# A second set of buffers for the second layer's regrouped queries, keys and values

## The chip, the cores and the metric

The kernel runs on one core of one Trainium2 chip. The metric is the device time of one execution in microseconds; the median of three runs before the change is 618.75 us (617.87 to 620.15). Changes within about half a per cent can't be told from none.

## The reference

Two transformer layers over 2,048 tokens (2 x 1024) of width 256. What matters here:

```python
# layer 0: causal attention, 32 heads of width 8, 8 key/value heads, T = 1024; then a gated FFN, fp8 inputs
q = (x @ Wq + bq).reshape(B, T, 32, 8).transpose(0, 2, 1, 3)
...
out = softmax(mask(q @ k.T / sqrt(8))) @ v @ Wo + bo
ffn = fp8dot(gelu(fp8dot(xn, w_gating[0])) * fp8dot(xn, w_gating[1]), w_linear)
x = x + out + ffn
# layer 1: attention *across the heads of a token*, 16 heads of width 16, no mask
scores = jnp.einsum('bshd,bstd->bsht', q, k) / jnp.sqrt(jnp.float32(HD))
weights = jax.nn.softmax(scores, axis=-1)
attn = jnp.einsum('bsht,bstd->bshd', weights, v)
# beside it a SiLU-gated FFN with RMS norm in the middle and ternary weights; x + both is the output
```

In the first layer the attention and the FFN both start from the same normed input. In the second layer the attention mixes only the 16 heads of one token, so every token is a small 16 x 16 attention of its own.

## The kernel before

The 2,048 tokens are 16 tiles of 128 (NT = 16). Every stage is a small function of a tile number, one set of functions per engine: `xnT.5` on TensorE turns tile 5's normed input, `qkv.5` projects it, and so on. The five lists in `ORDER` (lines 46 to 175) say in which order each engine issues these steps; each list is the program of its engine, so the engines run only in that order. Each step begins with its waits (`w.wait_ge`) on the semaphores that the other engines count up. The lists interleave the two layers and many tiles: while the first layer's attention of a late tile runs (`qk.Q`, `exp.Q`, `pv.Q`, 144 quads of score banks), the second layer of an earlier tile goes on beside it.

The second layer's attention of tile n goes through these steps, and these are what the change touches:

- TensorE `qkv1` (lines 737, 738) projects; ScalarE `qk1c` (L939), VectorE `ro1`, `ro2`, `v1c` (L1319 to L1328, L1306) and GpSimd `ro1p` (L1588, L1590) rotate and copy the result to `rqkv`, which has two copies.
- SyncE's queue: `vw` (L492) writes `rqkv` to a scratch tensor in HBM, and `vr` (L500, three DMAs) reads it back regrouped: each partition then holds one head of 8 tokens, 16 groups, in the buffer `G3` (queries, keys and values). There is one `G3`. So `vr(n)` waits for `PV1(n-1)`, the last reader of `G3`.
- TensorE `gT.2n` and `gT.2n+1` (L742) turn the queries and the keys of `G3`; VectorE `gTq` (L1335) and ScalarE `gTk` (L946) copy them to `qk1T`. There is one `qk1T`, so both wait for `S1(n-1)`.
- TensorE `S1` (L775) makes the scores of 8 tokens at a time. A pair of rows and columns in `G3` (written once by `cst`, L1026, from `ind1`) adds a large negative number where query and key are of different tokens. ScalarE `ex1` (L955) writes the exponentials to `stage`, of which there is one, and TensorE `PV1` (L786) multiplies them by the values.
- `o1r` (L1352), `o1T` (L795), `o1` (L1358, L1361) copy, turn and divide; SyncE's `ow` (L505) and `at1r` (L511) go through HBM again to bring the tokens back to partitions; `at1T` (L563, L564), `at1Tc` (L1403) and `wo1` (L807, L808) end it, and `yo` (L1409) adds the residual.

The second layer's FFN of the same tile is `gu` (L821, four parts), ScalarE `tg` (L964), VectorE `sg`, `hh` (L1368, L1377), then `ssq` (L970), `ssm` (L1383), `rsg` (L1597), `hxa` (L975), `hx` (L1389), and on TensorE `hxT` (L831), on VectorE `hTc` (L1397), on TensorE `dn1` (L840), and `yout` (L1419), the tile's output. Its buffers `h1`, `hx_b`, `hT` exist once.

All steps of TensorE but the scores and `pv` put their result in one of three PSUM banks (psA, psB, psC), in rotation: a step waits until the bank's content of three such steps before has been read (`shared`, `EMPTIED`).

At the end VectorE's `rng` (L1431 to L1441, nine small instructions) and a few more test whether the numbers stayed in the range in which the fast first pass is exact. If not, the kernel would run a second, wider pass; with these inputs it does not, and its code is not executed. The buffers `w8g`, `w8l` and `kTf` are as large as the second pass needs them. The first pass uses half of `w8g` and `w8l` (fp8 weights) and half of `kTf` (f16 keys).

GpSimd's `gz` (L1490 to L1493) fills the constant parts of `G3` once.

Of the kernel before, what the change touches and what calls it, by code (L numbers as in the profile page):

```python
# [7 lines left out]
ACT = mybir.ActivationFunctionType  # L8
# [9 lines left out]
NT = 16  # L18
# [273 lines left out]
def build(nc, A):  # L292
    ctx = ExitStack()
    with ctx:
# [90 lines left out]
        r1 = sb("r1", [128, 2, 512])  # L385
        rqkv = several(2, "rqkv", [128, 3, 256])
        G3 = sb("G3", [128, 3, 16, 32])
        qk1T = sb("qk1T", [128, 2, 4, 128])
        P1 = stage[:].rearrange("p (g n) -> p g n", n=128)
        rec1 = sb("rec1", [128, NT, 16])  # L390
        hl = sb("hl", [128, 12])
# [1288 lines left out]
```

## Time and profile before

| | |
|---|---|
| median of 3 runs | 618.75 us |
| the profiled execution | 618.31 us, of which its span is 616.5 us |
| TensorE busy | 567.0 us (92%) |
| ScalarE busy | 468.3 us (76%) |
| VectorE busy | 443.1 us (72%) |
| GpSimd busy | 249.9 us (41%) |
| mean granted TensorE clock | 0.987 |

The page gives for each engine the time in which it executed something. TensorE, VectorE and the others each work through their own list, and an idle stretch of one is put down to the instruction whose end released it. Idle time counts only on the engine that sets the end. The span runs from the first to the last instruction; the rest of an execution's time, here 1.8 us, lies around it. A step's name is found from the line, and its number by counting. In the windows view the columns are the stretch, its length, busy us of PE (TensorE matmul), PEld (weight load), DVE, ACT and POOL, each with its instructions, the granted TensorE clock, the DMA share and GB/s.

### The profile page before, as it was taken

What the parts mean: (1) busy time and instruction counts of PE and PEld (TensorE: products, weight loads), DVE (VectorE), ACT (ScalarE), POOL (GpSimd) and SP (SyncE); (2) the same over time, 40 slices, a digit from 0 to 9 for tenths busy, and PEclk for the clock granted to TensorE, in tenths of its full rate; (3) what the DMA queues carried; (4) which work ended last, traced back from release to release, by engine and by line L of the source; (5) the groups of instructions that cost most, each with busy time, mean ns of one, the idle gap of its engine ahead of it and who ended that gap; (6) DMA issues with size and microseconds to landing.
All of it is one profiled execution on the core that took longest, in us unless ns stands there. A gap on an engine that the chain in (4) does not pass through costs nothing. (4 is left out here: it accounts for less than half of the span.)

```text
span 616.5 us, 13198 instructions
## 1 busy us (share of the span) xinstructions
PE 567.0 (92%) x5085; PEld 290.5 (47%) x5085; DVE 443.1 (72%) x902; ACT 468.3 (76%) x605; POOL 249.9 (41%) x316
## 2 busy tenths in 40 slices
PE   3778989999999999999999999999999999999883
PEld 1333433445465545455344455654454444556562
DVE  5899989888877668766969666675646533677564
ACT  2489799988788898998697777778888978744240
POOL 3658736461444136415757462153231231242100
PEclk9699999999999999999999999999999999999998
DMA  8720110030412310311300021530403104054441
GB/s 283 271 69 2 35 36 1 1 52 7 65 43 35 53 27 11 52 20 18 61 1 2 27 27 44 88 44 27 61 2 61 18 1 70 15 97 79 70 54 45
DMA packets 150915, 30.41 MB, mean 49 GB/s; under 512 B 133952, under 2 KB 149568, under 8 KB 150848
## 3 DMA queue, kind: packets, MB, share of 16 engines
q1 hardware_dynamic: 150272, 29.19, 23.7%
q8 instruction: 42, 0.69, 0.5%
q10 hardware_dynamic: 576, 0.33, 0.3%
q14 instruction: 25, 0.20, 0.1%
HBM read 19.02 MB, written 10.49 MB: 48 GB/s over the span
## 5 line engine op out<-in xcount | busy, mean ns | idle before, releaser
L906 ACT ACTIVATE Pt<-psS 128x1024 f32<-128x1024 f32 x288 | 280.2, 1034 | 45.0 <-PE psS L658 28.2
L672 PE MATMUL psV<-Pt,vaug 128*32 128x512 f32 x1152 | 147.2, 602 | 1.1 <-DVE ob L1220 0.9
L1542 POOL TENSOR_SCALAR_AFFINE_SELECT Pt<-Pt 128x1024 f32<-128x1024 f32 x64 | 76.0, 1212 | 28.9 <-ACT Pt L906 28.5
L658 PE MATMUL psS<-qTf,kTf 32*128 32x512 f16 x576 | 71.1, 386 | 4.0 <-ACT Pt L906 2.8
L658 PEld LDWEIGHTS psS<-qTf,kTf 32*128 32x128 f16 x576 | 19.3, 91 | 78.4 <-ACT Pt L906 48.0
L672 PEld LDWEIGHTS psV<-Pt,vaug 128*32 128x32 f32 x1152 | 25.9, 108 | 45.6 <-issue 36.3
L1597 POOL TENSOR_TENSOR ss<-ss,mhalf 128x1 f32<-128x1 f32 x16 | 9.2, 577 | 91.4 <-DVE ss L1383 91.4
L955 ACT ACTIVATE stage<-psS 128x1024 f32<-128x1024 f32 x32 | 31.0, 1024 | 14.0 <-PE psS L775 14.0
L1571 POOL TENSOR_SCALAR rs<-mv 128x1 f32<-128x1 f32 x16 | 5.2, 323 | 69.8 <-DVE mv L1283 69.8
L1588 POOL TENSOR_TENSOR r<-qk,cos 128x256 f32<-128x256 f32 x16 | 12.4, 778 | 50.6 <-ACT qk L939 50.6
L1257 DVE SCALAR_TENSOR_TENSOR ga<-gw,gb 128x512 bf16<-128x512 f32 x32 | 26.2, 819 | 4.3 <-ACT gw L932 4.2
L1248 DVE SCALAR_TENSOR_TENSOR gw<-gw,gb 128x512 f32<-128x512 f32 x32 | 24.7, 772 | 6.2 <-ACT gw L921 6.1
L1533 POOL TENSOR_TENSOR QXf<-rt,QXf 128x512 f16<-128x512 f32 x16 | 19.1, 1191 | 23.2 <-ACT QXf L893 23.2
L1522 POOL TENSOR_TENSOR rt<-qkv,cs 128x320 f32<-128x320 f32 x16 | 16.3, 1017 | 29.9 <-DVE qkv L1119 27.5
L1578 POOL TENSOR_TENSOR xhs<-xn1T,xhs 128x256 f16<-128x256 f32 x16 | 12.0, 749 | 35.6 <-DVE xhs L1300 35.6
L1389 DVE SCALAR_TENSOR_TENSOR qtmp<-qtmp,ss 128x1024 f16<-128x1024 f32 x16 | 21.9, 1367 | 4.4 <-ACT qtmp L975 4.2
L1260 DVE TENSOR_TENSOR ga<-ga,fb 128x512 bf16<-128x512 bf16 x32 | 22.1, 690 | 3.7 <-DVE ga L1257 0.5
L821 PE MATMUL psB<-wguT,xhs 128*128 128x512 bf16 x92 | 23.7, 381 | 0.2
L970 ACT ACTIVATE qtmp<-qtmp 128x1024 bf16<-128x1024 f32 x16 | 16.9, 1058 | 8.3 <-PE psB L831 5.9
L975 ACT ACTIVATE qtmp<-qtmp,ss 128x1024 f16<-128x1024 f32 x16 | 18.5, 1156 | 6.0 <-POOL ss L1597 6.0
L932 ACT ACTIVATE gw<-gw 128x512 f32<-128x512 f32 x32 | 20.6, 644 | 2.0 <-DVE gw L1248 1.9
L821 PE MATMUL psC<-wguT,xhs 128*128 128x512 bf16 x84 | 21.6, 380 | 0.1
(345 smaller groups left out, 1294.5 us busy)
## 6 DMA issues: line engine op xcount, KB each, us to landing
qkvscr<-rqkv SPq DMA_DIRECT2D x16, 384.0 KB, 2.6
G<-qkvscr SPq DMA_DIRECT2D x48, 128.0 KB, 3.8
stage<-in_wg SPq DMA_DIRECT2D x4, 512.0 KB, 7.6
oscr<-o SPq DMA_DIRECT2D x16, 128.0 KB, 3.1
at<-oscr SPq DMA_DIRECT2D x16, 128.0 KB, 2.0
out<-yout SPq DMA_DIRECT2D x16, 128.0 KB, 2.8
x<-in_x SPq DMA_DIRECT2D x1, 1536.0 KB, 11.9
r<-in_wgu SPq DMA_DIRECT2D x2, 512.0 KB, 7.7
```

What stands on the lines that cost most here:

```text
L658: e.matmul(psS[j], kd[32 * j:32 * j + k, h, 128 * at:128 * at + 128], qd[32 * j:32 * j + k, 4 * h:4 * h + 4, :].rearrange("p s n -> p (s n ...
L672: ins = e.matmul(psV[32 * j:32 * j + 32, :], vaug[:, at, j, 32 * h:32 * h + 32], Pt[(4 * Q + j) % NP], start=(kb == 0 and h == 0), stop=(k ...
L821: ins = e.matmul(bank[:], src[:, pt, 128 * c:128 * c + 128], wguT[:, c, c0:c0 + 512], start=(k == 0), stop=(k == 3))
L906: e.activation(flat(Pt4[:, u % NP:u % NP + 2, :]), flat(psS4[:, j:j + 2, :]), ACT.Exp, scale=scale).then_inc(S["exp"], 1)
L932: e.activation(gw[:, half, :], gw[:, half, :], ACT.Tanh, scale=GC * GA).then_inc(S["th"], 1)
L955: e.activation(P1[:, 4 * b:4 * b + 8, :].rearrange("p g n -> p (g n)"), flat(psS4[:, b:b + 2, :]), ACT.Exp, scale=SC1).then_inc(S["ex1"], 1)
L1248: e.scalar_tensor_tensor(gw[:, half, :], gw[:, half, :], 1.0 / GA, gb[:, half, :], ALU.add, ALU.mult).then_inc(S["ge1"], 1)
L1257: e.scalar_tensor_tensor(a, gw[:, half, :], 1.0, gg, ALU.add, ALU.mult).then_inc(S["ge3"], 1)
L1260: e.tensor_tensor(a, a, fb[:, half, :], ALU.mult).then_inc(S["ge3"], 1)
L1389: e.scalar_tensor_tensor(hx_b[:, 1, :], h1, sn[:, 2:3], hx_b[:, 0, :], ALU.mult, ALU.subtract).then_inc(S["hx"], 1)
L1533: e.tensor_tensor(X4[:, 0:32, 2:4, :], heads(rt[n % len(rt)][:, 0, 0:256], 2), X4[:, 0:32, 0:2, :], ALU.subtract).then_inc(S["ql"], 1)
L1542: e.affine_select(out=p, in_=p, pattern=[[0, 8], [1, 128]], compare_op=ALU.is_ge, fill=0.0, base=0, channel_multiplier=-1).then_inc(S["mas ...
```

## The change

The odd tiles of the first pass get buffers of their own: `G3odd` (queries and keys) in the second half of `w8g`, `G3vodd` (values) in the second half of `w8l`, and `qk1Todd` in the second half of `kTf`. The functions `group` and `turned` choose by tile. The waits of `vr`, `gTk` and `gTq` go back by one tile: `vr(n)` now waits for `PV1(n-2)`, and the two copies for `S1(n-2)`. `gz` has two more memsets, `cst` one more wait and copy. The five lists in `ORDER` hold the same steps as before, in a new order almost everywhere; below are their ends, the start of GpSimd's, and parts of SyncE's.

```diff
--- before.py
+++ after.py
@@ ORDER["pe"], its end @@
 ...
-        "qk.142 pv.140 pv.141 gu.51 hxT.22 qk.143 dn1.10 hxT.23 S1.11 qkv1.26 xn1T.14 PV1.11 pv.142 pv.143 gu.52 "
-        "qkv1.27 gu.53 o1T.11 obT.15 gu.54 gT.24 gu.55 gT.25 gu.56 S1.12 attT.15 qkv1.28 PV1.12 at1T.11 wo0.15 "
-        "wo1.11 o1T.12 dn1.11 hxT.24 hxT.25 xn1T.15 qkv1.29 gT.26 gT.27 S1.13 gu.57 gu.58 PV1.13 at1T.12 qkv1.30 "
-        "o1T.13 wo1.12 gu.59 qkv1.31 gu.60 gT.28 gT.29 hxT.26 S1.14 dn1.12 PV1.14 hxT.27 at1T.13 o1T.14 wo1.13 gu.61 "
-        "dn1.13 hxT.28 gu.62 gT.30 gT.31 S1.15 gu.63 hxT.29 PV1.15 at1T.14 o1T.15 dn1.14 wo1.14 hxT.30 hxT.31 dn1.15 "
-        "at1T.15 wo1.15"),
 ...
+        "pv.139 pv.140 gu.51 xn1T.13 gT.23 qk.142 pv.141 hxT.22 hxT.23 xn1T.14 qk.143 gu.52 qkv1.26 qkv1.27 S1.11 "
+        "gu.53 pv.142 PV1.11 pv.143 o1T.11 gT.24 obT.15 gT.25 qkv1.28 attT.15 gu.54 gu.55 gu.56 wo0.15 at1T.11 S1.12 "
+        "wo1.11 dn1.11 qkv1.29 hxT.24 xn1T.15 hxT.25 PV1.12 gT.26 qkv1.30 o1T.12 gT.27 gu.57 S1.13 qkv1.31 gu.58 "
+        "gu.59 gu.60 PV1.13 gT.28 gT.29 o1T.13 at1T.12 S1.14 wo1.12 dn1.12 hxT.26 hxT.27 gT.30 gT.31 PV1.14 S1.15 "
+        "o1T.14 gu.61 at1T.13 PV1.15 wo1.13 o1T.15 gu.62 dn1.13 gu.63 hxT.28 hxT.29 at1T.14 wo1.14 dn1.14 at1T.15 "
+        "hxT.30 hxT.31 wo1.15 dn1.15"),
@@ ORDER["dve"], its end @@
 ...
-        "yo.13 hx.14 hh.30 yout.13 hTc.28 gTq.15 sg.31 hh.31 hTc.29 ssm.15 o1r.15 at1Tc.14 o1.15 hx.15 yo.14 yout.14 "
-        "hTc.30 hTc.31 rng.0 at1Tc.15 yo.15 yout.15"),
 ...
+        "gTq.14 at1Tc.12 o1.13 yo.12 yout.12 hTc.26 hTc.27 ssm.14 gTq.15 o1r.14 hx.14 o1.14 at1Tc.13 hh.30 o1r.15 "
+        "yo.13 o1.15 sg.31 yout.13 hh.31 hTc.28 at1Tc.14 ssm.15 hTc.29 yo.14 hx.15 at1Tc.15 yout.14 hTc.30 hTc.31 "
+        "yo.15 rng.0 yout.15"),
@@ ORDER["pool"], from its start @@
-        "zero.0 rs0.0 rs0.1 rs0.2 rs0.3 rope.0 ql.0 rope.1 mask.0 ql.1 mask.1 rope.2 ql.2 mask.4 mask.5 rs0.4 rope.3 "
-        "rs0.5 ql.3 gz.0 rope.4 mask.10 mask.11 xf.0 ql.4 xf.1 rs1.0 rs0.6 rope.5 mask.18 xl.0 mask.19 rs0.7 xf.2 "
 ...
+        "zero.0 rs0.0 rs0.1 rs0.2 rs0.3 rope.0 ql.0 rope.1 mask.0 ql.1 rs0.4 mask.1 rope.2 rs0.5 mask.4 ql.2 mask.5 "
+        "rope.3 ql.3 mask.10 rope.4 xf.0 mask.11 rs1.0 ql.4 xf.1 gz.0 rs0.6 rope.5 mask.18 xl.0 mask.19 xf.2 ro1p.0 "
+        "ql.5 rs0.7 rs1.1 rs1.2 rope.6 rsg.0 xl.1 mask.28 mask.29 rs0.8 ql.6 ro1p.1 xl.2 rs0.9 xf.3 ro1p.2 rs1.3 "
 ...
@@ ORDER["sp"], whole @@
-        "wg.2 wg.3 wt.2 wg.4 wt.3 wg.5 wt.4 wt.5 vw.0 vr.0 vw.1 ow.0 at1r.0 vr.1 vw.2 out.0 vr.2 ow.1 at1r.1 vw.3 "
 ...
-        "at1r.9 vw.11 ow.10 vr.11 at1r.10 vw.12 out.9 vr.12 out.10 ow.11 at1r.11 vw.13 vr.13 ow.12 out.11 vw.14 "
-        "at1r.12 vr.14 ow.13 vw.15 at1r.13 vr.15 ow.14 at1r.14 out.12 ow.15 out.13 at1r.15 out.14 out.15"),
+        "wg.2 wt.2 wg.3 wg.4 wg.5 wt.3 wt.4 wt.5 vw.0 vr.0 vw.1 ow.0 vr.1 at1r.0 vw.2 vr.2 out.0 ow.1 at1r.1 vw.3 "
 ...
+        "vr.7 out.4 ow.6 vw.8 out.5 at1r.6 vr.8 out.6 ow.7 vw.9 vr.9 at1r.7 ow.8 at1r.8 out.7 vw.10 out.8 vr.10 ow.9 "
+        "at1r.9 ow.10 at1r.10 vw.11 vr.11 vw.12 out.9 vr.12 ow.11 vw.13 at1r.11 vr.13 vw.14 vr.14 ow.12 vw.15 out.10 "
+        "at1r.12 vr.15 ow.13 at1r.13 out.11 ow.14 at1r.14 ow.15 out.12 out.13 at1r.15 out.14 out.15"),
@@ -386,6 +386,10 @@
         rqkv = several(2, "rqkv", [128, 3, 256])
         G3 = sb("G3", [128, 3, 16, 32])
         qk1T = sb("qk1T", [128, 2, 4, 128])
+
+        G3odd = flat(w8g[:]).bitcast(F32)[:, 1024:2048].rearrange("p (s g d) -> p s g d", s=2, d=32)
+        G3vodd = flat(w8l[:]).bitcast(F32)[:, 512:1024].rearrange("p (g d) -> p g d", d=32)
+        qk1Todd = flat(kTf[:])[:, 1280:2304].rearrange("p (s j n) -> p s j n", s=2, n=128)
         P1 = stage[:].rearrange("p (g n) -> p g n", n=128)
         rec1 = sb("rec1", [128, NT, 16])
         hl = sb("hl", [128, 12])
@@ -405,6 +409,18 @@
         yout_b = several(2, "yout", [128, 256])
         ysum = sb("ysum", [128, NT])
 
+        def odd(n):
+            return n < NT and n % 2 == 1
+
+        def group(n, s):
+
+            if not odd(n):
+                return G3[:, s, :, :]
+            return G3vodd if s == 2 else G3odd[:, s, :, :]
+
+        def turned(n, s):
+            return (qk1Todd if odd(n) else qk1T)[:, s, :, :]
+
         tst = [flat(r1[:]), qk1T[:].rearrange("p s j n -> p (s j n)")]
         filled, fills = shared_banks()
         scores_before = score_banks()
@@ -493,11 +509,11 @@
 
             def vr(n):
                 w.wait_ge(f"d_vw{n % 2}", 16 * (n // 2 + 1))
-                w.wait_ge("PV1", n)
-                w.wait_ge("gz", 2)
+                w.wait_ge("PV1", n - 1 if n < NT else n)
+                w.wait_ge("gz", 4 if odd(n) else 2)
                 src = qkvscr[n % NT].rearrange("s (g a) (b d) -> (a b) s g d", a=8, d=16)
                 for s in range(3):
-                    e.dma_start(G3[:, s, :, 0:16], src[:, s, :, :]).then_inc(S["d_vr"], 16)
+                    e.dma_start(group(n, s)[:, :, 0:16], src[:, s, :, :]).then_inc(S["d_vr"], 16)
 
             def ow(n):
                 w.wait_ge("o1", 2 * n + 2)
@@ -737,21 +753,21 @@
                 e.matmul(bank[:, 0:c1 - c0], src[:, 0, :], wqkv1[:, 0, c0:c1], start=True, stop=False)
                 e.matmul(bank[:, 0:c1 - c0], src[:, 1, :], wqkv1[:, 1, c0:c1], start=False, stop=True).then_inc(S["qkv1"], 1)
 
-            def transpose_groups(bank, s, sem):
+            def transpose_groups(bank, n, s, sem):
                 for j in range(4):
                     ins = e.transpose(bank[:, 128 * j:128 * j + 128],
-                                      G3[:, s, 4 * j:4 * j + 4, :].rearrange("p g d -> p (g d)"), identf[:])
+                                      group(n, s)[:, 4 * j:4 * j + 4, :].rearrange("p g d -> p (g d)"), identf[:])
                 ins.then_inc(S[sem], 1)
 
             def gT(m):
                 n, s = divmod(m, 2)
                 w.wait_ge("d_vr", 48 * (n + 1))
-                w.wait_ge("cst", 1)
-                transpose_groups(shared("gT", m), s, "gT")
+                w.wait_ge("cst", 2)
+                transpose_groups(shared("gT", m), n, s, "gT")
 
             def gTagain(n):
                 w.wait_ge("m1", 4 * (n - NT) + 4)
-                transpose_groups(shared("gTagain", n), 0, "gTagain")
+                transpose_groups(shared("gTagain", n), n, 0, "gTagain")
 
             def S1m(n):
                 w.wait_ge("gTq", n + 1)
@@ -772,8 +788,8 @@
                 for j in range(4):
                     for b in range(4):
                         scores_free("S1", n, b)
-                        ins = e.matmul(psS[b][:, 128 * j:128 * j + 128], qk1T[32 * b:32 * b + k, 1, j, :],
-                                       qk1T[32 * b:32 * b + k, 0, j, :], start=True, stop=True)
+                        ins = e.matmul(psS[b][:, 128 * j:128 * j + 128], turned(n, 1)[32 * b:32 * b + k, j, :],
+                                       turned(n, 0)[32 * b:32 * b + k, j, :], start=True, stop=True)
                         if j == 3:
                             ins.then_inc(S["S1"], 1)
 
@@ -783,7 +799,7 @@
                 bank = shared("PV1", n)
                 for c in range(4):
                     for j in range(4):
-                        ins = e.matmul(bank[32 * j:32 * j + 32, 128 * c:128 * c + 128], G3[:, 2, 4 * c + j, :],
+                        ins = e.matmul(bank[32 * j:32 * j + 32, 128 * c:128 * c + 128], group(n, 2)[:, 4 * c + j, :],
                                        P1[:, 4 * j + c, :], start=True, stop=True)
                 ins.then_inc(S["PV1"], 1)
 
@@ -941,9 +957,9 @@
             def gTk(n):
                 w.wait_ge("tc", 12)
                 w.wait_ge("gT", 2 * n + 2)
-                w.wait_ge("S1", 4 * n)
+                w.wait_ge("S1", 4 * (n - 1) if n < NT else 4 * n)
                 bank = psM[filled["gT", 2 * n + 1] % len(psM)]
-                e.activation(qk1T[:, 1, :, :].rearrange("p j n -> p (j n)"), bank[:], ACT.Copy).then_inc(S["gTk"], 1)
+                e.activation(turned(n, 1).rearrange("p j n -> p (j n)"), bank[:], ACT.Copy).then_inc(S["gTk"], 1)
 
             def ex1(n):
                 w.wait_ge("w8", 6)
@@ -1024,6 +1040,9 @@
                 w.wait_ge("d_c", 96)
                 w.wait_ge("gz", 2)
                 e.tensor_copy(G3[:, 0:2, :, 16:24],
+                              ind1[:].unsqueeze(2).to_broadcast([128, 2, 16, 8])).then_inc(S["cst"], 1)
+                w.wait_ge("gz", 4)
+                e.tensor_copy(G3odd[:, :, :, 16:24],
                               ind1[:].unsqueeze(2).to_broadcast([128, 2, 16, 8])).then_inc(S["cst"], 1)
 
             def w8(k):
@@ -1331,8 +1350,8 @@
                 bank = psM[filled["gT", 2 * n] % len(psM)]
                 w.wait_ge("tc", 12)
                 w.wait_ge("gT", 2 * n + 1)
-                w.wait_ge("S1", 4 * n)
-                e.tensor_copy(qk1T[:, 0, :, :].rearrange("p j n -> p (j n)"), bank[:]).then_inc(S["gTq"], 1)
+                w.wait_ge("S1", 4 * (n - 1) if n < NT else 4 * n)
+                e.tensor_copy(turned(n, 0).rearrange("p j n -> p (j n)"), bank[:]).then_inc(S["gTq"], 1)
 
             def m1(n):
                 for b in range(4):
@@ -1491,6 +1510,8 @@
                 w.wait_ge("gz", 1)
                 e.memset(G3[:, 1, :, 24:25], 1.0)
                 e.memset(G3[:, 2, :, :], 1.0).then_inc(S["gz"], 1)
+                e.memset(G3odd, 0.0).then_inc(S["gz"], 1)
+                e.memset(G3vodd, 1.0).then_inc(S["gz"], 1)
 
             def w8a(k):
                 src = stage[:, 1024 * (k % 2):1024 * (k % 2) + 1024]
```

## Rows read from the trace of the kernel before

**Rows 1.** Windows view: busy us (x instructions) per engine, five stretches.

```profile
0.00:60.00 60.00, 40.95 (x268) 17.77 (x268) 50.97 (x103) 37.01 (x50) 36.61 (x53) 0.91 0.49 161
60.00:150.00 90.00, 83.46 (x682) 37.19 (x682) 80.17 (x155) 80.26 (x109) 48.32 (x59) 1.00 0.10 22
150.00:540.00 390.00, 382.79 (x3523) 195.25 (x3520) 262.35 (x538) 324.90 (x413) 151.88 (x188) 1.00 0.21 35
540.00:594.40 54.40, 48.98 (x508) 32.31 (x508) 38.13 (x79) 21.97 (x30) 12.58 (x17) 1.00 0.52 81
594.40:616.50 22.10, 10.83 (x113) 7.98 (x109) 11.49 (x30) 4.12 (x5) 0.55 (x1) 0.86 0.15 34
```

**Rows 2.** Waits of TensorE, 0 to 60 us: total, times, longest.

```profile
PE psC L612 <- DVE QXf L1150: 2.4, 1, 2.4
```

**Rows 3.** Waits of TensorE from 544.8 to 594.4 us, all that the view names.

```profile
PE psS L775 <- ACT qk1T L946: 1.6, 2, 0.8
PE psA L563 <- DMA at<-oscr: 0.9, 1, 0.9
PE psA L831 <- DVE stmp L1368: 0.6, 1, 0.6
PE psC L786 <- ACT stage L955: 0.5, 2, 0.3
PE psC L737 <- DVE o L1361: 0.5, 1, 0.5
PE psA L737 <- DVE stmp L1397: 0.5, 1, 0.5
PE psA L795 <- DVE stmp L1368: 0.4, 1, 0.4
PE psA L807 <- DVE at1T L1403: 0.3, 1, 0.3
```

**Rows 4.** Timeline of TensorE, late (start us, us, line, idle before).

```profile
542.90 1.90 PE L672 MATMUL psV<-Pt,vaug 128*32 128x512 f32 x16
...
566.08 1.17 PE L775 MATMUL psS<-qk1T 24*128 24x128 f32 x32 [0.78 <-ACT qk1T L946]
...
583.44 1.08 PE L786 MATMUL psC<-stage,G 128*32 128x128 f32 x32 [0.26 <-ACT stage L955]
...
591.38 0.60 PE L742 MATMUL psC<-identf,G 128*128 128x128 f32 x4
...
594.43 1.04 PE L821 MATMUL psB<-wguT,xhs 128*128 128x512 bf16 x4
...
604.43 1.92 PE L840 MATMUL psB<-wpT,stmp 128*128 128x256 bf16 x16 [0.95 <-DVE stmp L1397]
```

**Rows 5.** Timeline of SyncE's queue, late.

```profile
578.03 0.36 SPq L492 DMA_DIRECT2D qkvscr<-rqkv  x1
...
584.63 2.62 SPq L500 DMA_DIRECT2D G<-qkvscr  x3
```

**Rows 6.** Timeline of VectorE, the last tile and the range test.

```profile
599.81 1.27 DVE L1389 SCALAR_TENSOR_TENSOR qtmp<-qtmp,ss 128x1024 f16<-128x1024 f32 x1
...
604.29 0.67 DVE L1431 TENSOR_REDUCE hl<-rec 128x1 f32<-128x512 f32 x1
...
606.72 0.41 DVE L1403 COPY at1T<-psC 128x256 f32<-128x256 f32 x1
...
608.88 0.42 DVE L1419 TENSOR_TENSOR yout<-psB,yo 128x256 f32<-128x256 f32 x1
```

**Rows 7.** Timeline of GpSimd at 56 us: the fill of the buffer.

```profile
56.51 0.95 POOL L1490 MEMSET G<- 128x1024 f32 x1
...
57.56 0.67 POOL L1493 MEMSET G<- 128x512 f32 x1
```

**Rows 8.** VectorE at the same time: one cast.

```profile
56.89 0.85 DVE L1264 CAST a<-ga 128x512 fp8e4<-128x512 bf16 x1
```

**Rows 9.** The same cast over the span (ns min/median/max).

```profile
L1264 DVE CAST a<-ga x32: 426/427/1326, 40.8 to 486.9; 128x512 fp8e4<-128x512 bf16 x32
```

233 rows, old and new, of the table ORDER are left out of this document.

## The prediction

> **What bounds the kernel now.** I read the windows view first. TensorE is busy 382.8 of the 390 us from 150 to 540 us, 98%; ScalarE has 324.9 there, VectorE 262.4, GpSimd 151.9 [rows 1]. So TensorE sets the time, and what an order or a buffer can give back is its idle time, 49.5 us in all: 19.0 us to 60 us, 6.5 to 150, 7.2 to 540, 5.4 to 594.4, and 11.3 behind that [rows 1]. The first 8 us wait for the input and the last 7 follow the last output, which the change doesn't touch. The stretch behind the last `pv` is the one to look at: it ends at 544.80 us (542.90 + 1.90), and the last `yout` ends at 609.30 (608.88 + 0.42) [rows 4, 6], so it takes 64.5 us. In it the first layer is over, nothing fills gaps but the second layer of tiles 11 to 15, and each tile's attention goes through HBM twice.
>
> The waits view of that stretch names eight groups of waits of TensorE, 5.3 us together, up to `gu.63` [rows 3]. None is for the regrouped data itself. The wait that the change takes away does bind on SyncE's queue: `vw.15` is issued at 578.03 us, `vr.15` only at 584.63, 0.1 us after `PV1.14` ended (583.44 + 1.08) [rows 4, 5]. But `gT.30`, which reads the result, starts at 591.38 with no wait before it [rows 4]: the list had put other work there. So the removed wait is worth nothing by itself; it is worth what the new lists make of it. What they pay now for the late `vr` is that `gT` stands right before its `S1`: S1.13 waits 0.78 us for the copy of the turned keys, S1.15 the same [rows 3, 4].
>
> **Part by part, first the end.** The new TensorE list has 62 steps behind `pv.143`, the old 65: `gu.52`, `qkv1.27` and `gu.53` now stand before it. At 0.9 us each (a `gu` takes 1.04 us with its overlap [rows 4]) these 2.7 us change sides of a point up to which TensorE is full either way: no gain. The old tail to compare with is 64.5 - 2.7 = 61.8 us.
>
> Up to the start of `gu.63` (594.43 [rows 4]) the old list takes 49.6 us, less 2.7 is 46.9. In the new one `PV1.15` (1.0) and `o1T.15` (0.45) have moved ahead of it and `hxT.28` (0.45) behind: +1.0. Of the waits of 5.3 us I go through the new order one by one.
> - S1.13 and S1.15 (1.6): now `gu.57` and `PV1.14`, 0.9 to 1.0 us, stand between gT and S1; the wait was 0.78 each. Gone.
> - PV1 on ScalarE's exponentials (0.5): three or more steps stand between S1 and PV1 for tiles 12 to 14. Gone.
> - The bank waits of hxT (0.6), of the two qkv1 (0.5 and 0.5) and the o1T.11 one (0.4), wo1.13 (0.3): the step that used the bank before has now 0.8 to 2.5 us more of other steps behind it. Gone.
> - at1T.12 on its DMA (0.9): `at1r.12` stands now behind `vw.15`, which needs `qkv1.31`, and only some five steps lie between. Stays.
> - New: PV1.15 has 1.7 us of work behind S1.15, while the two exponentials need 2.1: 0.4.
>
> So 4.4 of 5.3 go, 0.9 stay, 0.4 is new. VectorE runs a fixed list too, and some of its copies will stand behind a waiting one that I can't place from the list: bounds 0 and 4.4 (all comes back); I take 1.6, nearer to the lower, as the longest of the present waits is 0.9. Together 46.9 - 5.3 + 1.0 + 2.9 = 45.5 us.
>
> From `gu.63` to the end of `yout.15` the old kernel takes 609.30 - 594.43 = 14.9 us. It loses there to the range test: the nine instructions from 604.29 to 606.72 stand before the copy `at1T.15`, so `wo1.15`, the last product, starts 2.4 us late [rows 6]. The new list puts `rng` behind `yo.15` and before `yout.15`, and `dn1.15` last. The chain is then: `hx.15` ends 6.65 us behind the start of gu.63 (599.81 + 1.27 - 594.43), hxT.31 0.45, its copy 0.7, yo 0.4, range test 2.4, yout 0.4, hand-overs 0.3: 11.3 us. dn1.15, at most 1.9 us [rows 4], is done before the range test. That is 3.6 less. The new tail is 45.5 + 11.3 = 56.8 against 61.8: -5.0 us.
>
> **The start and the middle.** In the first 60 us one wait that is no start-up wait stands out, 2.4 us of qxT.4 for the rotated keys of tile 2 [rows 2]. The old list has only obT.0, qk.4, qkv.3, pv.3 and qk.5 before it; the new one adds up.4 to up.7 and attT.0 there. VectorE's table of angles (`tab`) also moves from before q0.2 to after tile 2. Both help, but the `up` steps depend on the same busy VectorE (51.0 of 60 us [rows 1]). Bounds: -2.4 and, if w8 weights come later because wt.2 now goes ahead of wg.3, +2. I take -0.8. From 60 to 540 us TensorE idles 13.7 us of 480 [rows 1]. The 11 first `S1` stand at the same `qk` as before (S1.5 behind qk.91 in both lists, for example), so the second set brings nothing there. The rest of the reordering can give or take a part of this: bounds -4 and +6, taken 0.
>
> **What is added.** Two memsets on GpSimd, the size of those of 0.95 and 0.67 us [rows 7], and one VectorE copy, about 0.3 to 0.4 by the 256-column copy of 0.41 [rows 6]. GpSimd is idle 41.7 of the 90 us in which they now fall [rows 1], so they cost nothing unless `rope.5` behind them becomes late: bounds 0 and 1.6 + 0.4, taken +0.3. While the old memsets ran, a cast on VectorE took 0.85 us instead of its usual 0.43 [rows 7 to 9]. The Trainium skill, "SBUF — State Buffer", section "SBUF: two separate sides", speaks against the change here: VectorE and GpSimd share a port pair, and the one that starts first keeps it for its whole instruction while the other is blocked. The row agrees with it, with 0.42 us lost. By the rule alone two memsets could stop VectorE for all of their time, and the sum would be some 1.3 us higher, 614.1.
>
> The sum: -5.0 - 0.8 + 0 + 0.3 = -5.5 us. The profiled execution takes 618.31 us, its span 616.5 and 1.8 around it; 618.3 - 5.5 = 612.8 us. The median of the three runs is 0.4 above the profiled one, which is inside what runs differ by.
>
> **The rivals.**
> 1. *The tail gives it back.* The FFN buffers of layer two exist once: hh.30 waits for hx.14, and hx.14 now stands on VectorE behind ssm.14, which stands behind hTc.27. If that chain sets the pace, none of the waits before gu.63 is saved; there is 1.0 more work, and only the 3.6 of the last chain remain, in part: 616.5 us (615.2 to 621.4). For it: the old waits are spread over eight causes, of which only S1's 1.6 has to do with the buffers. Against it: TensorE had 49.0 busy of 54.4 us there [rows 1], so no chain has been in charge for long. Chance 0.22.
> 2. *Slower, by the bank rotation in the middle.* Nearly every TensorE step there needs the bank of three steps before, read by VectorE or ScalarE in their own lists. If the new lists don't meet as well, the idle share of 1.8% from 150 to 540 us becomes 4%: +8.6 us, and with half of the tail's gain 618.3 + 8.6 - 2.5 = 624. It decides the sign from 5.5 us more idle time on. For it: all five lists are new almost everywhere; against it, the share is low all along and no rule of the order has changed. Chance 0.15.
> 3. *The second set isn't used at all.* If vr is held by its data, not by PV1, in the new order too, gT comes no earlier and only the moved range test counts: 618.3 - 3.6 = 614.7. It lies within my forecast's range; I give it 0.12 of that.
> 4. *The start gains fully.* The 2.4 us go, the tail's waits go with nothing in return (1.6 less), and the middle gives 1 to 2: 607.5. Chance 0.08.
>
> **How the numbers follow.** My forecast (610 to 615.2, with the third rival in it) has 0.55. Half a per cent, 3.1 us, is about what can be told from no change. Faster by more: 0.55 + 0.08 = 0.63; within: 0.22; slower: 0.15. The range cuts off half of the fourth and most of the second rival, and takes in the first: 609 to 620.5.
>
> **What would show it.** Right: in the new trace the stretch from the end of the last pv to the end of the last yout is 57 us (55 to 59); S1.13 to S1.15 wait under 0.3 us; two vr are issued before the PV1 of the tile before; the range test lies beside dn1.15; TensorE's idle time from 150 to 540 us is 5 to 9 us. Wrong: a tail over 60 us (then the first rival, seen as waits of hh or hTc), over 12 us idle in the middle (the second), or TensorE waits of over 1 us behind the new memsets near rope.5.

## The result and the profile after

The changed kernel takes 610.3 us (median, 609.8 to 611.8) against 619.15 in the same comparison: ratio 0.9857, 95% interval 0.9836 to 0.9877, so 8.85 us or 1.4% faster. Forecast were 612.8 us, range 609 to 620.5. The direction and the range hold; the gain is 8.85 us where 5.5 were summed. The profiled execution takes 610.33 us, its span 608.6.

The windows view of the changed kernel, with the stretches of [rows 1]:

```profile
0.00:60.00 60.00, 37.87 (x258) 16.52 (x260) 50.29 (x96) 34.64 (x48) 35.69 (x49) 0.91 0.47 161
60.00:150.00 90.00, 84.01 (x694) 39.72 (x702) 80.67 (x161) 83.38 (x113) 52.79 (x62) 1.00 0.11 26
150.00:540.00 390.00, 381.31 (x3467) 195.44 (x3497) 265.05 (x544) 326.59 (x416) 157.22 (x193) 1.00 0.22 35
540.00:594.40 54.40, 51.29 (x585) 35.38 (x592) 41.65 (x82) 23.87 (x31) 12.24 (x15) 1.00 0.47 79
594.40:608.60 14.20, 5.18 (x47) 3.89 (x44) 7.95 (x22) 0.03 (x1) 0.00 (x0) 0.86 0.07 23
```

The page of the kernel before counts 5085 products of TensorE and as many weight loads; here there are 5040 products against 5085 loads. So 45 records of products are missing, 38 of them of `gu`, and TensorE's busy time is too low by them (many a `gu` shows as three products instead of four). The count of loads per stretch is the safer measure. In the 54.4 us from 540 us TensorE loads weights 592 times where it did 508 times, and in the first 60 us 260 where it did 268.

I compare further by work. Each step is known by its place in the list and its first weight load; each kind is weighted by its median time from its first load to that of the next step, over both traces; then one reads when the changed kernel has done as much as the old one. Worked out so, not lines of a view, and good to about a microsecond:

```
time in kernel before        60    150    350    540    570    590    607 us
changed kernel is later by  2.6   -0.5   -2.3   -3.0   -3.2   -5.3   -7.9 us
```

The end of the chain is the tail. The last `pv` of the changed kernel ends at 545.7 us (544.64 + 1.06), and `yout.15` at 601.42:

```profile
544.64 1.06 PE L688 MATMUL psV<-Pt,vaug 128*32 128x512 f32 x8 [0.44 <-POOL Pt L1563]
...
565.86 1.17 PE L791 MATMUL psS<-kTf 24*128 24x128 f32 x32
...
570.61 1.08 PE L802 MATMUL psA<-stage,w8l 128*32 128x128 f32 x32
571.62 0.66 PE L758 MATMUL psB<-identf,G 128*128 128x128 f32 x4
...
584.25 1.08 PE L802 MATMUL psA<-stage,w8l 128*32 128x128 f32 x32 [0.44 <-ACT stage L971]
...
589.49 0.81 PE L837 MATMUL psC<-wguT,xhs 128*128 128x512 bf16 x3
...
596.56 0.61 PE L847 MATMUL psB<-identh,qtmp 128*128 128x128 f16 x8 [0.70 <-DVE yout L1438]
...
598.12 1.92 PE L856 MATMUL psA<-wpT,stmp 128*128 128x256 bf16 x16
```

These are, of TensorE's timeline: the last pv, S1.13, PV1.13 and directly behind it gT.28, PV1.15, gu.63, hxT.31 and dn1.15. The first product of gu.63 has no record; its first weight load has:

```profile
589.17 0.64 PEld L837 LDWEIGHTS psC<-wguT,xhs 128*128 128x128 f16 x4
```

So gu.63 is taken to start at 589.17 us. S1.13, which waited 0.78 us [rows 4], doesn't wait. gT.28 starts as PV1.13 ends. The waits of the stretch from 545.7 to 589.3 us, where [rows 3] had 5.3 us, are now 1.3, all the view names:

```profile
PE psA L802 <- ACT stage L971: 0.4, 1, 0.4
PE psA L811 <- DVE o1r L1371: 0.4, 1, 0.4
PE psB L753 <- DVE stmp L1416: 0.3, 1, 0.3
PE psB L758 <- DVE stmp L1416: 0.2, 1, 0.2
```

SyncE's queue shows why gT.28 need not wait. `vr.14` (L516) is issued at 561.95 us, 8.7 us before PV1.13 starts, and `vr.15` at 571.80; in [rows 5] `vr.15` stood until PV1.14 had ended. The same holds earlier: of the tiles 1 to 11, seven (2, 3, 4, 6, 7, 8 and 10) have their `vr` issued 2.9 to 30 us before the end of the PV1 of the tile before; in the old trace none has.

```profile
559.40 0.36 SPq L508 DMA_DIRECT2D qkvscr<-rqkv  x1
561.95 2.64 SPq L516 DMA_DIRECT2D G<-qkvscr  x3
...
568.58 0.36 SPq L508 DMA_DIRECT2D qkvscr<-rqkv  x1
...
571.80 1.76 SPq L516 DMA_DIRECT2D w8g<-qkvscr  x2
```

And the end on VectorE, beside [rows 6]: hx.15, the range test (first instruction), yout.15. The test runs beside dn1.15 but outlasts it: dn1.15 ends at 600.04.

```profile
594.46 1.28 DVE L1408 SCALAR_TENSOR_TENSOR qtmp<-qtmp,ss 128x1024 f16<-128x1024 f32 x1 [0.76 <-ACT qtmp L991]
...
598.46 0.68 DVE L1450 TENSOR_REDUCE hl<-rec 128x1 f32<-128x512 f32 x1
...
601.00 0.42 DVE L1438 TENSOR_TENSOR yout<-psA,yo 128x256 f32<-128x256 f32 x1
```

### The profile page after: what moved, and what is told of

It reads as the page before. It is cut to its first block, busy times and chain, and to the rows that moved or that the text cites. A ratio compares the mean times of both kernels' runs of the same rounds, so it can differ in the third digit from the quotient of the medians.

```text
span 608.6 us, 13144 instructions
## 1 busy us (share of the span) xinstructions
PE 559.7 (92%) x5040; PEld 290.9 (48%) x5085; DVE 445.6 (73%) x903; ACT 468.5 (77%) x605; POOL 257.9 (42%) x318
## 4 chain that ended last, share of the span: by engine, by line
PE 66%; DVE 13%; ACT 9%; issue 6%; DMA 2%; POOL 1%; SPq 0%; DVEq 0%; ACTq 0%; POOLq 0%
PE psV L688 16%; PE psS L674 7%; ACT Pt L922 5%; PE psA L837 3%; PE psS L791 3%; PE psC L837 2%; PE psB L837 2%; DMA stage<-in_wg 1%; PE psA L725 1%; PE psA L856 1%; PE psC L753 1%; PE psB L753 1%; PE psC L754 1%; DVE ga L1276 1%; DMA x<-in_x 1%
## 5 line engine op out<-in xcount | busy, mean ns | idle before, releaser
L1563 POOL TENSOR_SCALAR_AFFINE_SELECT Pt<-Pt 128x1024 f32<-128x1024 f32 x64 | 74.5, 1188 | 41.7 <-ACT Pt L922 41.5
L674 PE MATMUL psS<-qTf,kTf 32*128 32x512 f16 x576 | 72.4, 386 | 5.0 <-DVE qTf L1184 2.5
L1554 POOL TENSOR_TENSOR QXf<-rt,QXf 128x512 f16<-128x512 f32 x16 | 21.4, 1339 | 35.3 <-ACT QXf L909 35.1
L1609 POOL TENSOR_TENSOR r<-qk,cos 128x256 f32<-128x256 f32 x16 | 13.0, 810 | 43.5 <-ACT qk L955 43.5
L1276 DVE SCALAR_TENSOR_TENSOR ga<-gw,gb 128x512 bf16<-128x512 f32 x32 | 29.1, 910 | 1.6 <-ACT gw L948 1.6
L1267 DVE SCALAR_TENSOR_TENSOR gw<-gw,gb 128x512 f32<-128x512 f32 x32 | 26.1, 815 | 1.7 <-ACT gw L937 1.7
L1546 POOL TENSOR_TENSOR rt<-qkv,sn 128x160 f32<-128x160 f32 x32 | 23.4, 751 | 0.0
L837 PE MATMUL psB<-wguT,xhs 128*128 128x512 bf16 x77 | 20.5, 379 | 2.0 <-issue 1.4
L837 PE MATMUL psA<-wguT,xhs 128*128 128x512 bf16 x75 | 19.8, 379 | 2.2 <-issue 1.0
L1283 DVE CAST a<-ga 128x512 fp8e4<-128x512 bf16 x32 | 20.9, 654 | 1.1
```

Of the source, the lines that this page charges most:

```text
L674: e.matmul(psS[j], kd[32 * j:32 * j + k, h, 128 * at:128 * at + 128], qd[32 * j:32 * j + k, 4 * h:4 * h + 4, :].rearrange("p s n -> p (s n ...
L837: ins = e.matmul(bank[:], src[:, pt, 128 * c:128 * c + 128], wguT[:, c, c0:c0 + 512], start=(k == 0), stop=(k == 3))
L1267: e.scalar_tensor_tensor(gw[:, half, :], gw[:, half, :], 1.0 / GA, gb[:, half, :], ALU.add, ALU.mult).then_inc(S["ge1"], 1)
L1276: e.scalar_tensor_tensor(a, gw[:, half, :], 1.0, gg, ALU.add, ALU.mult).then_inc(S["ge3"], 1)
L1546: e.tensor_tensor(rb[:, :, :, ev], pairs[:, :, :, 1 - ev], snv[:, :, ev].unsqueeze(1).to_broadcast([128, 40, 4]), ALU.mult).then_inc(S["ro ...
L1554: e.tensor_tensor(X4[:, 0:32, 2:4, :], heads(rt[n % len(rt)][:, 0, 0:256], 2), X4[:, 0:32, 0:2, :], ALU.subtract).then_inc(S["ql"], 1)
```

## The experiments

Each time is the median of 12 executions (numbers 1, 3 and 4), of 5 or 6 (2 and 5 to 8) or of 4 (9 and 10). The kernel before took 619.61 us beside 1 to 4, 618.96 beside 5 to 8 and 620.39 beside 9 and 10, so differences of a microsecond between numbers are not to be trusted. The lists are cut in the edits shown.

**1. The buffers with the old order.**

```diff
 ORDER = {
-    (the five new lists)
+    (the five lists of the kernel before)
 }
```

> The second set and the earlier waits, with the five old lists. Theory A (the gain is in the new order; the removed wait by itself is worth nothing, because the old lists have other work between it and gT): same as before, 619 us within 1.5. Rival B (SyncE's wait for PV1 held the tail, so the data's earlier arrival pays by itself): 613 to 616 us. Rival C (the two added memsets and the copy cost): 620 to 621 us, with a wait of TensorE behind rope.4.

Measured: 619.65 against 619.61 us, ratio 1.0005 (0.9994 to 1.0017). The second set by itself is worth nothing that can be measured. Seven of the eight groups of waits in its tail are those of [rows 3], with the same lengths, among them:

```profile
PE psS L788 <- ACT kTf L959: 1.6, 2, 0.8
PE psA L844 <- DVE stmp L1384: 0.6, 1, 0.6
PE psC L799 <- ACT stage L968: 0.5, 2, 0.3
```

although `vr.15` is issued 2.9 us before the start of PV1.14 (583.18 against 586.05 us):

```profile
583.18 1.45 SPq L513 DMA_DIRECT2D w8g<-qkvscr  x2
```

The eighth, the 0.9 us of at1T.12 for its DMA, isn't there. That DMA took 3.6 us from issue to landing instead of 4.5, and 2.3 in the changed kernel, so this need not be the second set's doing. A transfer that lands earlier helps nobody whose place in the list stays where it was. So A holds and B is refuted. C isn't quite excluded, since a cost of up to 1 us lies inside the interval, but its sign, a new wait of TensorE near the memsets, is not in the trace.

**2. The new order with one set of buffers.** Six gT can't stand where the new list has them, since the buffer they read is filled only behind the PV1 that follows them there; they had to move.

```diff
-... 'gT.8' ... 'gT.9' ... 'PV1.3' ... 'gT.12' ... 'PV1.5' ... 'gT.14' ... 'PV1.6' ... 'gT.30' 'gT.31' 'PV1.14' ...
+... 'PV1.3' 'gT.8' 'gT.9' ... 'PV1.5' 'gT.12' ... 'PV1.6' 'gT.14' ... 'PV1.14' 'gT.30' 'gT.31' ...
-                w.wait_ge("PV1", n - 1 if n < NT else n)
+                w.wait_ge("PV1", n)
 (and all the rest of the second set: buffers, memsets, copy, and the waits of gTq and gTk)
```

> The five new lists with one set of buffers and the old waits. Six gT steps (8, 9, 12, 14, 30, 31) that the new TensorE list has ahead of the PV1 before them had to go right behind it, and gTq.4, gTq.6 and gTq.15 right behind the o1r there. Theory A (order, of which only a few places need the second set): 611.5 to 614 us, 1 to 4 above the changed kernel, with waits of 5 to 6 us for the data before gT.8 and gT.30 partly filled. Rival D (the second set carries the gain): 617 us or more. Rival E (the set is not needed at all): 610 to 611 us.

Measured: 670.8 us, ratio 1.0846 (1.082 to 1.0871), 60 us above the changed kernel. Its waits of TensorE for the regrouped data are 39.8 us in nine places:

```profile
PE psB L739 <- DMA G<-qkvscr: 19.6, 4, 5.7
PE psA L739 <- DMA G<-qkvscr: 10.9, 2, 5.5
PE psC L739 <- DMA G<-qkvscr: 9.3, 3, 5.8
```

That was far outside what I expected of theory A, and rival D (617 us or more) is what came: the new order can't do without the second set. I had thought of a few places only.

**3 and 4. Half new, half old.** Number 3 has the new lists for what the changed kernel had begun by 525 us and the old order for the rest; number 4 has the old lists for what the kernel before had begun by 528 us and the new order for the rest. Both have the second set. All five lists are joined so; "pe" stands for them.

```diff
-    "pe": (new list)
+    "pe": (new list up to 525 us, then the remaining steps in the old order)      # 3
+    "pe": (old list up to 528 us, then the remaining steps in the new order)      # 4
```

> The changed kernel's lists for all that it had begun by 525 us, and behind that the rest of the steps in the old order. By the comparison of the same work in the two traces the tail is worth 5.9 us. Theory A (start, middle and tail add up): 615 to 617.5 us. Rival F (the tail's gain comes from how the middle leaves the engines): 611 to 613 us.

> The old lists for all that the kernel before had begun by 528 us, and behind that the rest in the new order, with the second set. Theory A (the parts add up): 612.5 to 614.5 us, 5 to 6 below the kernel before. Rival F (the tail's gain needs the new middle): 616 us or more.

Measured: 617.0 (ratio 0.9964, 0.9951 to 0.9977) and 618.2 us (0.9987, 0.9974 to 1.0). Number 3 came as theory A had it: start and middle of the new order give 2.6 us, and the tail the other 6.2 of the 8.85. Number 4 missed: 1.4 us instead of 5 to 6. By work, it loses 3.5 us from 520 to 550 us, where the two orders are joined, and gains 6.6 from there to the end. Its waits show part of the join, 1.66 us of a `gu` for VectorE's copy of the turned queries:

```profile
531.38 0.70 PE L820 MATMUL psB<-wo,at1T 128*128 128x256 f32 x2 [0.52 <-DVE at1T L1419]
534.17 1.04 PE L834 MATMUL psC<-wguT,xhs 128*128 128x512 bf16 x4 [1.66 <-DVE kTf L1351]
```

So in the trace the tail's gain is there without the new middle, but a join of two orders costs as much as such a run wants to measure. By its time alone, rival F (616 us or more) is what came; against it speaks only the comparison by work, in which the new tail does gain, behind the join.

**5. The old start.**

```diff
-    "pe": (new list)
+    "pe": (old list up to 62 us, then the remaining steps in the new order)
```

> The changed kernel with the old lists for all that the kernel before had begun by 62 us, the new order behind that. By the same work in the two traces the new start is 3.3 us behind at 75 us. Theory A (the new start costs and the rest of the order doesn't need it): 607.5 to 609 us. Rival G (the join of two orders costs as much again, as 2 to 3 us of waits at the join of the kernel with the new tail): 610 to 613 us.

Measured: 613.3 us, ratio 0.9908 (0.9886 to 0.993), 3 us worse than the new start. That is rival G, by its range. It can't say what the new start costs, since the join is in it; it says only that this cure is dearer. All five lists are joined here too.

**6. The range test in two parts.**

```diff
+    n == 0, before yo.12:   max and min of rec, max of widest
+    n == 1, before yout.15: max and min of rec1, the three comparisons, the minimum
-    rng.0 before yout.15:   all nine
```

> The changed kernel with the range test in two parts: the three reductions that need only the first layer stand before yo.12, the other six instructions before yout.15. In the changed kernel's trace the test holds yout.15 from 600.04, when dn1.15 is done, to 601.00. Theory A: 0.9 us less, 609.4 us. Rival H (nothing, since the first part delays a copy that TensorE waits for): 610.3 us.

Measured: 610.1 us, ratio 0.9859 (0.9836 to 0.9881), not told from the changed kernel's. In its trace it does what was wanted: from the start of dn1.15 to that of yout.15 there are 1.96 us, where the changed kernel has 2.88.

```profile
599.06 1.92 PE L854 MATMUL psA<-wpT,stmp 128*128 128x256 bf16 x16
```
```profile
601.02 0.42 DVE L1436 TENSOR_TENSOR yout<-psA,yo 128x256 f32<-128x256 f32 x1 [0.36 <-PE psA L854]
```

The profiled run as a whole is no faster because it reaches gu.62 at 587.61 us, 0.94 later than the changed kernel's 586.67. That isn't the edit: by work it is as late at 540 us already, and the first part of the test runs only at 575.73. So rival H's reason, a copy delayed by the first part, isn't seen, and the 0.9 us are saved in this trace. The median doesn't show them; its interval is 1.4 us to either side, and whether the kernel is really faster stays open.

**7. The fp8 weights first.**

```diff
-        "wg.2 wt.2 wg.3 wg.4 ..."
+        "wg.2 wg.3 wt.2 wg.4 ..."
```

> The changed kernel with wg.3 ahead of wt.2 again on SyncE's queue, as in the old list. The trace shows the cast w8.3 waiting 1.0 us for that load and up.0 0.8 us for the cast, with qkv.2 5.6 us later than before. Theory A (the late fp8 weights are a cause of the slow start): 1 to 2 us less, 608.5 to 609.3. Rival I (what is saved there is waited for elsewhere in the first 150 us): 610.3 within 0.5.

Measured: 610.6 us, ratio 0.9857 (0.9834 to 0.988), no difference. Rival I: the late weights show in the trace of the changed kernel, but their 0.8 us isn't the cause of the slower start.

**8. The old end.**

```diff
-    "pe":  ... hxT.29 at1T.14 wo1.14 dn1.14 at1T.15 hxT.30 hxT.31 wo1.15 dn1.15
+    "pe":  ... hxT.29 at1T.14 wo1.14 dn1.14 hxT.30 hxT.31 dn1.15 at1T.15 wo1.15
-    "dve": ... hx.15 at1Tc.15 yout.14 hTc.30 hTc.31 yo.15 rng.0 yout.15
+    "dve": ... hx.15 yout.14 hTc.30 hTc.31 rng.0 at1Tc.15 yo.15 yout.15
```

> The changed kernel with the old order of the last steps: dn1.15 before at1T.15 and wo1.15 on TensorE, the range test before the copy at1Tc.15 on VectorE. The prediction put 3.6 us of the gain on the last chain. Theory A: 2.5 to 3.6 us more, 613 to 614. Rival J (the test lay beside dn1.15 before as well; only wo1.15 and yo.15 behind dn1.15 are dearer): 1 to 2 us more, 611.3 to 612.3.

Measured: 612.6 us, ratio 0.9897 (0.9877 to 0.9916), 2.3 us above the changed kernel: between the ranges of theory A (from 613) and rival J (up to 612.3), so the time doesn't decide. The trace sides with J's reason. On VectorE the test (598.32 to 600.84) lies beside dn1.15 here too, and the copy at1Tc.15 behind it is only some 0.2 us late, for at1T.15 itself ends at 600.60:

```profile
598.46 1.92 PE L853 MATMUL psB<-wpT,stmp 128*128 128x256 bf16 x16 [1.36 <-DVE stmp L1413]
600.22 0.27 PE L576 MATMUL psC<-identf,at 128*128 128x128 f32 x1
600.33 0.27 PE L577 MATMUL psC<-identf,at 128*128 128x128 f32 x1
601.23 0.70 PE L820 MATMUL psA<-wo,at1T 128*128 128x256 f32 x2 [0.63 <-DVE at1T L1419]
```

What costs is that at1T.15, its copy, wo1.15 and yo.15 stand in a row behind dn1.15, on an input that was there before it. In front of it they fit into the wait for hTc.31, 1.36 us here. From gu.63 to the end of yout.15 this trace takes 13.5 us and the changed kernel's 12.25, so 1.2 us of the 2.3 are seen in the end itself; the rest is not placed.

**9 and 10. One set for some tiles only.** The old waits for tiles 0 to 11 (9) or from 12 on (10), in the new order, with those of the gT moved as in number 2 that lie in that part (8, 9, 12 and 14 in number 9, 30 and 31 in number 10).

```diff
-                w.wait_ge("PV1", n - 1 if n < NT else n)
+                w.wait_ge("PV1", n - 1 if n < NT and n > 11 else n)      # 9; in 10: n <= 11
-                w.wait_ge("S1", 4 * (n - 1) if n < NT else 4 * n)
+                w.wait_ge("S1", 4 * (n - 1) if n < NT and n > 11 else 4 * n)      # 9, in gTk and gTq; in 10: n <= 11
```

> The changed kernel in which vr, gTk and gTq of tiles 0 to 11 wait as before the change, for PV1 and S1 of the tile before; the buffers stay two. gT.8, 9, 12, 14 and gTq.4, gTq.6 are moved behind PV1 and o1r as in the one-set run. That run was 51 us slower and waited 40 us for the regrouped data in nine places. Theory K (the new lists lean on the second set in the middle too, against the prediction): 635 us or more. Rival L (the middle doesn't use it, as predicted): 612 us or less.

> The same for tiles 12 to 15 only; gT.30 and gT.31 stand behind PV1.14, gTq.15 behind o1r.14. Each gT then starts right behind the PV1 it waits for, so the three DMAs and their landing, 5.7 us, lie open where no other step is left between. Theory K (both parts of the list lean on it, the sum of the two is the 51 us): 625 to 632 us. Rival M (only the tail leans on it): 650 us or more.

Measured: 639.2 (ratio 1.0315, 1.0294 to 1.0336) and 642.5 us (1.0353, 1.0334 to 1.0372). That is 28.9 and 32.2 us above the changed kernel, 61.1 together (59.1 by the ratios, as the kernel before was slower beside these two), and number 2 is 60.5 above. The two parts add up within that, and the middle leans on the second set about as much as the tail: theory K; for number 10 it is even 10 us more than K's range. This is what these lists would lose without the set, not what the set gains in either part. In the tail of number 10 three gT wait for a whole trip of the data:

```profile
573.10 1.11 PE L755 MATMUL psA<-identf,w8g 128*128 128x128 f32 x4 [5.31 <-DMA w8l<-qkvscr]
...
590.21 1.12 PE L755 MATMUL psB<-identf,G 128*128 128x128 f32 x4 [5.34 <-DMA G<-qkvscr]
...
609.07 1.12 PE L755 MATMUL psB<-identf,w8g 128*128 128x128 f32 x4 [5.73 <-DMA w8l<-qkvscr]
```

## Why the prediction was right or wrong

**The bound and the place were right.** TensorE sets the time before and after, and the largest part of the gain lies behind the last pv: 55.7 us from the end of the last pv to the end of yout.15 (601.42 - 545.70), forecast were 56.8, the comparable old value was 61.8. The other signs came too: S1.13 to S1.15 have no wait that the view names, `vr` is issued ahead, the range test lies beside dn1.15, and TensorE idles 8.7 us from 150 to 540 us (5 to 9 were named), less what the missing records hide. Number 3 measures the tail without that reading: 617.0 - 610.3 = 6.7 us by its medians, 6.2 by what is left of the whole.

**The waits of the tail were right in kind.** Of the eight groups of 5.3 us, 4.4 were to go, and 0.9 of at1T.12, 0.4 of PV1.15 and 1.6 unplaced to remain. 1.3 us are left; PV1.15 has its 0.4; at1T.12 doesn't wait, as its DMA landed 2.3 us behind its issue and not 4.5. From the last pv to gu.63 it is 43.5 us (589.17 - 545.70) against 45.5 forecast. The term that was too large is the 1.6 for waits that couldn't be placed.

**"The range test costs 2.4 us" was wrong.** I read 2.4 us from the span of the test in [rows 6] and took all of it for lateness of wo1.15. But the copy had nothing to copy for most of that time: at1T.15 stood behind dn1.15, and ends at 606.56 us in the kernel before, 0.16 before the copy starts (606.72 [rows 6]):

```profile
606.29 0.27 PE L564 MATMUL psC<-identf,at 128*128 128x128 f32 x1
607.19 0.70 PE L807 MATMUL psA<-wo,at1T 128*128 128x256 f32 x2 [0.63 <-DVE at1T L1403]
```

What the new end saves is a row of steps behind the last large product. In the old kernel they could hardly have stood in front of it, for their input was late: `at1r.15` was issued at 602.99 us and landed at 605.04, behind the start of dn1.15 at 604.43. In the changed kernel PV1.15 is done 12 us earlier and `at1r.15` is issued at 591.67, 6.4 us before dn1.15:

```profile
602.99 0.32 SPq L511 DMA_DIRECT2D at<-oscr  x1
```
```profile
591.67 0.33 SPq L527 DMA_DIRECT2D at<-oscr  x1
```

From gu.63 to the end of yout.15 the changed kernel takes 12.25 us, not 11.3: 2.6 less than the 14.9 before, where 3.6 were forecast. The 0.9 that the sum lacked is mostly the 0.70 us that hxT.31 waits for the `yout` of tile 14, which holds its bank and stands on VectorE behind hx.15 and at1Tc.15. So the tail of 55.7 us is a sum of errors that partly cancel: 2.0 too much up to gu.63, 0.9 too little behind it.

**"The second set brings nothing in the middle" was wrong,** and this is the step that failed in its reason. I had compared where S1 stands among the qk, found it the same for eleven tiles, and concluded that the middle doesn't use the set. What matters is where gT stands against the PV1 of the tile before. In us from the end of PV1(n-1) to the start of gT.2n, worked out from both traces:

```
tile n                        2     3     4     6     7     8     9    10    12    13    14    15
kernel before               7.6  12.4   8.1  11.5   7.2   9.0   7.8   7.4   6.6   7.0   7.5   6.9
changed kernel              5.9   7.9 -16.2  -4.9  -1.9   4.3   9.3   2.8   2.4  -0.1  -0.1  -2.6
```

Tiles 1, 5 and 11 have 16 us and more in both. In the old list no gT starts earlier than 6.6 us behind it, and the three DMAs take 5.1 to 6.4 us there from issue to the last landing; so the old order keeps clear of that trip in all 15 tiles, and the trace showed no wait for it anywhere. The new list goes below 6.6 in ten tiles, six of them in the middle. Numbers 9 and 10 show what each half would cost without the set. The forecast for the middle was 0 (-4 to +6); number 3 gives 2.6 us for start and middle together, against 0.5 forecast for both with the additions. Whether those 2.6 come from the set or from the rest of the new order is not shown: no run has a good order for one set in the middle.

**The start: the term was wrong up to 60 us, and its net size stays open.** Forecast was -0.8. At 40 us, by work, all eight profiles with the new start (the changed kernel's and those of numbers 2, 3 and 6 to 10) are 2.3 to 3.3 us behind the kernel before, and the three other profiles with the old start (numbers 1, 4 and 5) are within 0.5 of it. It isn't the fp8 weights (number 7). The wait of 2.4 us in [rows 2] is gone, and others of 3.3, 2.1 and 2.5 us have come:

```profile
PE psB L628 <- DVE QXf L1169: 3.3, 1, 3.3
PE psS L674 <- DVE qTf L1184: 2.5, 2, 1.4
PE psA L725 <- DVE attT L1255: 2.1, 1, 2.1
```

But the old start isn't that much better in the end. In the profiles of numbers 1, 4 and 5 TensorE runs at the lower of its two clock levels (1.2 and 2.4 GHz, 0.50 and 1.00 in the view) for 3.4 us right behind that wait of 2.4 us, and for 3.4 us again at 62 us. The profile of the kernel before has the same wait and neither of these stretches. (Of the eight with the new start, three have one stretch of 3.4 us, at 49 us.) Here for number 1, then for the kernel before:

```profile
44.90:48.30 3.40, 3.31 (x26) 2.04 (x26) 3.10 (x6) 2.67 (x4) 2.18 (x3) 0.50 0.00 0
62.00:65.40 3.40, 3.40 (x18) 0.90 (x20) 2.47 (x4) 2.85 (x4) 2.46 (x4) 0.50 0.16 29
```
```profile
44.90:48.30 3.40, 3.37 (x46) 2.02 (x44) 3.30 (x7) 3.30 (x6) 2.40 (x2) 1.00 0.00 0
```

So at 75 us numbers 1, 4 and 5 are 2.1 to 3.4 us behind, too, and those with the new start 2.6 to 3.8; at 150 us the latter are at -0.7 to +0.5, numbers 1 and 4 still at 2.2 and 2.5. The profile of the kernel before was a lucky one in this stretch, and a comparison of two single profiles overstates what the new start loses. No timed run confirms a loss. My upper bound was +2. What the lists then win back between 60 and 540 us by work, 5.6 us, I can't put down to single waits.

**What was added** was put at +0.3; number 1 finds nothing, within 1 us. The blocking that the prediction read from [rows 8] isn't seen beside the new memsets either: they run from 85.20 to 86.75 us in the changed kernel, and the instructions of VectorE beside them, of 0.43, 0.42 and 0.18 us, have their usual lengths.

**The rivals.** The first (the tail gives it back) and the second (the bank rotation in the middle) didn't come. The third (the set isn't used) is refuted by numbers 2, 9 and 10. The fourth (607.5) came in part: the time lies midway between it and the forecast, the unplaced waits of the tail are gone and the middle gives something, but not the start.

The four combinations put it shortly:

```
                 one set      two sets
old order       619.6 us     619.65 us
new order       670.8 us     610.3 us
```

Neither part does anything good alone. The entry at the lower left has six steps of TensorE moved to make it run, so it isn't the best order for one set; the old order is likely nearer to that.

## What to carry to other kernels

A wait that doesn't show in a trace may still be what the order was built around: measure the distance between the step that frees a buffer and the first step that needs it filled again, for every tile, and compare it with the transfer's trip. If the distance is never less than the trip, as here, a second buffer may be worth something, but only together with an order that uses it; the buffer alone gave nothing here. And before a side job is called the cause of a late step, look when that step's input was there.

## What the runs showed of the hardware

- The trip of regrouped data through the queue (three DMAs of 128 KB each, from issue to the last landing) takes 5.1 to 6.6 us in the traces of the kernel before, the changed one and numbers 2, 9 and 10. In number 2 it lies open as 5.3 to 5.8 us in the six places where a gT stood right behind the step that frees the buffer, and as 0.85, 2.6 and 2.9 us in three where some steps lay between.
- The long stalls of TensorE cost more here than themselves. In number 2, seven of the nine waits have the lower clock level in their last part or right behind them: it sets in between 3.5 us before the wait's end and 0.6 us behind it, lasts 3.4 to 10.2 us, and makes 51 us in all, with TensorE busy in 36.5 of them; the mean granted clock is 0.948, where the changed kernel has 0.988. Two of these stretches, and S1.13 and S1.14, the same work at either level:

```profile
267.60:274.40 6.80, 5.31 (x22) 3.60 (x23) 2.57 (x5) 3.31 (x5) 0.00 (x0) 0.50 0.21 35
632.80:643.00 10.20, 6.71 (x49) 5.03 (x50) 2.66 (x4) 3.57 (x4) 0.00 (x0) 0.50 0.43 59
```
```profile
606.77 1.17 PE L772 MATMUL psS<-qk1T 24*128 24x128 f32 x32
...
622.09 2.09 PE L772 MATMUL psS<-qk1T 24*128 24x128 f32 x32
```

- An estimate from these rows accounts for what the three kernels lose beyond their waits: at half the clock, half of TensorE's busy time in such stretches is lost. Spans of the profiled executions, in us:

```
                                                 number 2   number 9   number 10
span above the changed kernel's                      59.1       28.6        33.0
waits of TensorE for the regrouped data              39.8       19.7        19.3
half of its busy time at the lower level             18.3        8.3        14.0
left                                                  1.0        0.6        -0.3
```

- The fall of the clock isn't the same each time. A wait of 2.9 us before gT.24 had none behind it in number 2 and 6.8 us of it in number 10; the wait of 2.4 us in [rows 2] had none in the kernel before and 3.4 us in number 1.
